# Moving one-hot comparisons and a rotation to GpSimd, taking softmax denominators from a ones column, and loading the output weights at a later point

## What is computed

```python
x = x + quantised_matmul(layernorm(x), ctx_4096)                 # L0 xattn
x = x + attention(layernorm(x), wq, bq, wk, bk, wv, bv)          # L0 attn: rotation of q and k, softmax(qk)v, 32 heads of 32
x = x + lora_ffn(layernorm(x), A, B, Wr)                         # L0 ffn: 64 experts, top 16, rank 16
x = x + knn_gather(ctx_4096[:, :2], layernorm(x), w, b)          # L1 xattn: 16 nearest of 1024 points, affine mix
x = x + causal_attention(layernorm(x), Wq, Wk, Wv) @ Wo          # L1 attn
x = x + lora_ffn1(layernorm(x), route_w, A, Bw)                  # L1 ffn: 8 experts, top 1
```

## Time and profile before

| | |
|---|---|
| median of 3 runs | 310.29 us (309.75 to 310.63) |
| profiled execution: device time | 308.52 us |
| profiled execution: span from first to last instruction | 306.7 us |
| PE busy | 221.6 us, 72% (1909 matmuls) |
| PEld busy | 135.4 us, 44% |
| DVE busy | 215.5 us, 70% (394 instructions) |
| ACT busy | 73.7 us, 24% |
| POOL busy | 26.4 us, 9% (29 instructions) |
| chain that ended last, by engine | PE 47%, DVE 34%, ACT 6%, issue 5%, DMA 4%, POOL 2% |
| mean granted TensorE clock | 0.80 of full speed |

### The profile page before, as it was taken

How to read it: one execution, slowest core, us unless ns; L and a number is a source line. 1 busy time by engine, 2 the same in 40 slices (tenths; PEclk the granted TensorE clock), 3 DMA queues, 4 the chain that set the end, 5 groups by cost and what they waited for, 6 DMA issues and landing times.

```text
span 306.7 us, 4506 instructions
## 1 busy us (share of the span) xinstructions
PE 221.6 (72%) x1909; PEld 135.4 (44%) x1909; DVE 215.5 (70%) x394; ACT 73.7 (24%) x112; POOL 26.4 (9%) x29
## 2 busy tenths in 40 slices
PE   0037443699997849669997993667729998989664
PEld 0021110333475727456444453667724476854251
DVE  0767997897998699989997978469860244911223
ACT  0439621100008235843217021000001013510010
POOL 7143470100000000010000001000010000000000
PEclk9999557559999756976999997775955999559976
DMA  4698999930004416606719674991000000000001
GB/s 135 183 332 300 370 416 343 388 151 0 2 0 139 138 51 191 178 0 235 316 40 409 248 266 156 362 410 39 6 0 0 0 0 2 2 2 0 0 0 68
DMA packets 18941, 45.09 MB, mean 147 GB/s; under 512 B 3829, under 2 KB 9079, under 8 KB 17898
## 3 DMA queue, kind: packets, MB, share of 16 engines
q1 hardware_dynamic: 17764, 44.12, 40.1%
q10 hardware_dynamic: 1158, 0.69, 0.8%
HBM read 44.16 MB, written 0.64 MB: 146 GB/s over the span
## 4 chain that ended last, share of the span: by engine, by line
PE 47%; DVE 34%; ACT 6%; issue 5%; DMA 4%; POOL 2%; SPq 1%; POOLq 0%; DVEq 0%
PE pair L352 16%; PE pair L547 5%; PE pair L491 5%; PE pair L527 4%; DVE knn_d L768 3%; DVE idx L763 3%; DVE idx L776 3%; DVE v L772 3%; DVE v L759 3%; PE pair L292 2%; DMA bufX<-in_ctx 2%; PE dist_ps L284 2%; DVE ring L809 2%; DVE bufY L847 2%; PE dist_ps L527 2%
## 5 line engine op out<-in xcount | busy, mean ns | idle before, releaser
L352 PE MATMUL pair<-are,xnT 128*128 128x256 f32 (+1 forms) x96 | 34.0, 502 | 0.0
L284 PE MATMUL dist_ps<-knn_rows 24*128 24x512 bf16 x32 | 11.6, 447 | 24.5 <-DMA knn_rows<-sq_scratch 20.1
L352 PEld LDWEIGHTS pair<-are,xnT 128*128 128x128 f32 x96 | 18.7, 204 | 13.9 <-issue 12.5
L1095 POOL TENSOR_SCALAR veps<-mv 128x1 f32<-128x1 f32 x6 | 1.4, 226 | 246.5 <-DVE mv L744 246.5
L759 DVE MAX8 v<-dist_ps 128x8 f32<-128x1024 f32 x16 | 19.5, 1221 | 3.7 <-PE dist_ps L284 3.6
L444 PE MATMUL pair<-arc,xnT 128*128 128x512 bf16 x32 | 14.0, 597 | 10.3 <-POOL arc L1103 9.6
L677 ACT COPY xnT<-pair 128x512 f32<-128x512 f32 x8 | 4.6, 586 | 69.5 <-PE pair L292 69.4
L292 PE MATMUL pair<-cst,xn 128*128 128x128 f32 x40 | 8.3, 376 | 16.5 <-DVE xn L750 16.5
L772 DVE MAX8 v<-knn_d 128x8 f32<-128x1024 f32 x16 | 19.5, 1221 | 0.2
L763 DVE FIND_INDEX8 idx<-v,dist_ps 128x8 uint32<-128x1024 f32 x16 | 19.6, 1223 | 0.0
L776 DVE FIND_INDEX8 idx<-v,knn_d 128x8 uint32<-128x1024 f32 x16 | 19.5, 1218 | 0.0
(11 more groups left out here) (171 smaller groups left out, 373.5 us busy)
## 6 DMA issues: line engine op xcount, KB each, us to landing
ring<-in_ctx SPq DMA_DIRECT2D x8, 1024.0 KB, 6.4
are<-in_L_attn_wq SPq DMA_DIRECT2D x1, 4096.0 KB, 14.9
ring<-in_L_ffn_A SPq DMA_DIRECT2D x4, 1024.0 KB, 13.4
are<-lo_scratch SPq DMA_DIRECT2D x4, 1024.0 KB, 7.7
ard<-in_L_attn_Wq SPq DMA_DIRECT2D x1, 4096.0 KB, 14.1
ring<-lo_scratch SPq DMA_DIRECT2D x4, 1024.0 KB, 4.7
arc<-in_L_attn_Wo SPq DMA_DIRECT2D x1, 4096.0 KB, 18.6
are<-in_L_attn_wk SPq DMA_DIRECT2D x1, 1024.0 KB, 17.4
```

Source lines behind the costliest of these rows:

```text
L284: m = mm(bank[h][:, :], q, knn_R[:, b, h * HALF:(h + 1) * HALF], start=True, stop=True)
L352: m = mm(o, xnTk[:, k, :], w(k), start=(l == 1 and k == 0), stop=(k == KT - 1))
```

## The change

- GpSimd now runs all eight `onehot` calls (same operation, same operands): 0 to 5 behind `power(2)`, then `power(3)`, then 6 and 7, then `power(4)` and `power(5)`.
- The rotation of L0 is on GpSimd, four `tensor_tensor` for each of three calls. ScalarE first copies q and k from PSUM into `xn`, the third copy behind the first rotation, whose input it overwrites. TensorE waits for the first of these copies before it reuses bank 4. L1 keeps its rotation on VectorE.
- V gets a 33rd column of ones in each of its 8 groups, so the product with the probabilities also gives their sum, in both layers. The reductions L864 and the reciprocal L867 go. Instead VectorE takes two reciprocals of 8 values from PSUM for each half of the heads, and the scaling is two `tensor_tensor` of 256 values where it was four of 128.
- SP waits for the sixth pick before it loads `Wo`.

```diff
             sp.wait_ge(sem("ffn0_filled"), 2)
+            sp.wait_ge(sem("picked"), PAIRS - 2)
             load(Wo, A["L1_attn_Wo"].rearrange("(k p) n -> p k n", p=P), "ld_wo")
...
                 if prep_a:
                     pe.wait_ge(sem("ld_wr"), 16)
+                    pe.wait_ge(sem("qk_copied"), 1)
...
                         g = 4 * (c // 2) + r
-                        o = (2 * g + c % 2) * DH
+                        o = (4 * (c // 2) + 2 * (r % 2) + c % 2) * OW
...
-                                       vsb[S * dup:S * dup + S, b, g * DH:(g + 1) * DH], start=True, stop=True)
+                                       vsb[S * dup:S * dup + S, b, g, :], start=True, stop=True)
...
+            for i, (o, n) in enumerate(((0, HALF), (HALF, HALF), (0, DKV))):
+                act.wait_ge(sem("k_filled") if i == 2 else sem("q_filled"), 1 if i == 2 else i + 1)
+                if i == 2:
+                    act.wait_ge(sem("rope_done"), 1)
+                cp(xn[:, o:o + n], bank[4 + i][:, 0:n]).then_inc(sem("qk_copied"), 1)
             attention(0, (0, 8, (2, 3)), (8, 8, (6, 7)))
...
                 for h in range(2):
-                    dve.wait_ge(sem("q_filled"), 2 * l + h + 1)
-                    rope(bank[4 + h], h * HALF, 4)
+                    if l:
+                        dve.wait_ge(sem("q_filled"), 2 * l + h + 1)
+                        rope(bank[4 + h], h * HALF, 4)
                     for t in mid[h]:
                         advance(t)
...
-                for r in range(4):
-                    dve.wait_ge(sem("probs_ready"), 4 * l + r + 1)
-                    ins = v.tensor_reduce(sdv[:, r], bufY[:, r * HALF:(r + 1) * HALF].rearrange("p (a j m) -> p a j m", a=2, j=4),
-                                          AX.X, ALU.add)
-                link(ins)
-                link(v.reciprocal(smx[:, :], sden[:, :]))
                 for t in late[1:]:
                     advance(t)
 
                 for n in range(2):
                     dve.wait_ge(sem("attn_filled"), 2 * l + n + 1)
...
                     for u in range(2):
-                        b = bank[(2 if n else 6) + u].rearrange("p (a n g d) -> p n a g d", a=2, n=2, g=4)[:, n]
-                        for a in range(2):
-                            ins = v.tensor_tensor(ov[:, a, :, u, :], b[:, a], rd[:, a, :, u].unsqueeze(2).to_broadcast([P, 4, DH]),
-                                                  ALU.mult)
+                        ins = v.reciprocal(rden[:, 2 * n + u, :], got[u][:, :, DH])
+                    link(ins)
+                    for u in range(2):
+                        ins = v.tensor_tensor(ov[:, u], got[u][:, :, 0:DH].rearrange("p (a g) d -> p a g d", a=2),
+                                              rden[:, 2 * n + u, :].rearrange("p (a g) -> p a g", a=2).unsqueeze(3)
+                                              .to_broadcast([P, 2, 4, DH]), ALU.mult)
...
             index_parts(3)
-            onehot(0)
...
             normalise(3)
-            onehot(1)
-            onehot(2)
-            onehot(3)
...
                 pick(p)
-                if p < 4:
-                    onehot(4 + p)
...
             g.memset(knn_R[:, :, :], 1.0).then_inc(sem("knn_rows_set"), 1)
+            g.memset(vsb[:, :, :, :].rearrange("p b g d -> p (b g d)"), 1.0).then_inc(sem("v_ones"), 1)
...
+            def onehot(q):
+
+                b, c = q // 4, q % 4
+                pool.wait_ge(sem(f"row_done{q}"), 16)
+                a = LOb[b][:, 4096 * c:4096 * c + 4096]
+                g.tensor_scalar(a, a, pcol, None, ALU.is_equal).then_inc(sem("onehot_ready"), 1)
...
-            for n in range(1, 6):
-                power(n)
+            power(1)
...
+                nc.gpsimd.tensor_tensor(a, ps, table(cosb, DH), ALU.mult).then_inc(sem("rope_part"), 1)
+                nc.gpsimd.tensor_tensor(dst[:, :, :, 0:hd], ps[:, :, :, hd:DH], table(sinb[:, 0:hd], hd), ALU.mult).then_inc(sem("rope_part"), 1)
+                nc.gpsimd.tensor_tensor(dst[:, :, :, hd:DH], ps[:, :, :, 0:hd], table(sinb[:, hd:DH], hd), ALU.mult).then_inc(sem("rope_part"), 1)
+                parts[0] += 3
+                pool.wait_ge(sem("rope_part"), parts[0])
+                nc.gpsimd.tensor_tensor(flat, flat, prod, ALU.add).then_inc(sem("rope_done"), 1)
+
+            for i, (o, n, j) in enumerate(((0, HALF, 4), (HALF, HALF, 4), (0, DKV, 1))):
+                pool.wait_ge(sem("qk_copied"), i + 1)
+                rope(xn[:, o:o + n], i * HALF, j)
+            power(2)
+            for q in range(6):
+                onehot(q)
+            power(3)
+            onehot(6)
+            onehot(7)
+            power(4)
+            power(5)
```

More of the change, by code:

```diff
@@ L28 @@
 DKV = KV * DH
+VW = DH + 1
+OW = DH + 2
 NPTS = 1024
@@ L111, in build @@
         rstd = sb("rstd", [P, 3])
-        smx = sb("smx", [P, H])
-        sden = sb("sden", [P, H])
+        rden = sb("rden", [P, 4, 8])
         v8 = sb("v8", [P, 4, 8])
@@ L872, in attention @@
                     dve.wait_ge(sem("attn_filled"), 2 * l + n + 1)
[L873 to L874 removed]
+                    ov = xn[:, :].rearrange("p (a n g u d) -> p n u a g d", a=2, n=2, g=4, u=2)[:, n]
+                    got = [bank[(2 if n else 6) + u][:, 0:8 * OW].rearrange("p (s d) -> p s d", d=OW) for u in range(2)]
                     for u in range(2):
[L876 to L879 removed]
+                        ins = v.reciprocal(rden[:, 2 * n + u, :], got[u][:, :, DH])
[4 more added lines that the diff above has]
+                                              .to_broadcast([P, 2, 4, DH]), ALU.mult)
                     if l:
```

30 lines of the change are left out of this document (17 added, 13 removed).

## The result

The changed kernel takes 352.47 us (median of 4 runs, 351.81 to 353.93) against 310.02 for the kernel before on the same chip: a ratio of 1.139, interval 1.132 to 1.145. It is 42 us slower; the forecast was 4.3 us slower, with a range that ended at 320. The profiled execution took 353.93 us, 45.4 more than the profiled execution of before.

A forecast was written before the change was run, and what follows sets the result against it. Bound by a chain: VectorE to 158.7 us, TensorE and ScalarE to 182, VectorE's norm and table, then TensorE's gather. Terms -1.95, +7.2, -1.4, +4.4, -4.2, +0.2 sum to +4.3 on 310.29: 314.6 us, range 303 to 320.

The forecast's parts named there:

- the length of a one-hot on GpSimd: GpSimd's 4096-value comparison, scaled from a 2048-value tensor_scalar of 1.90 us: 3.6 us, bounds 1.8 and 7.
- The third rival: Comparison on GpSimd slower: at 5 us each 323 us, at about 7 us each 335 us; chance 0.12.
- Rotation, 0: L0 rotation moved to GpSimd: ends by 91 us, ahead of `dist(7)`, so no gain or loss.
- Denominators in L0, -1.95: L0 attention: reductions and old reciprocal leave VectorE's chain, `xn` comes earlier; 1.95 us gained.
- One-hots 0 to 3, +7.2: GpSimd one-hots hold VectorE at L986 and the index split: +7.2 us, net +5.3 at `dist(14)`.
- One-hots 4 and 5, nothing: One-hots of pairs 4 and 5 on GpSimd end by 182, before `power(3)` at 190: no cost.
- Table, -1.4: Before the gather: one-hots 1 to 3 no longer stand between `xn` and the table copy; 1.4 us gained.
- One-hots 6 and 7, +4.4: On GpSimd after `power(3)`, they hold VectorE's norm and table, so the gather starts later: +4.4 us.
- Gather, -4.2: TensorE's gather stalls, read as instruction fetch beside loads, shrink from 7.6 to 3.4 us with `Wo` later; bounds 0 and 7.
- Denominators in L1, +0.2: L1 attention: TensorE can't use the earlier first half; new reciprocals follow the last product: +0.2 us.
- Blocking in one place only: Rival 2: VectorE blocked in one of two places, most likely at one-hots 0 to 3: 310.2 us; chance 0.12.
- hardly at all: Rival 1: blocking small, one-hots of 1.8 us or small instructions that pass: 303.0 us; chance 0.16.

The follow-up runs named there:

- the last two kernels: One-hots on VectorE where it waits, 0 to 4 ahead of the picks, three weight loads later: 300.21 us; the same with L0 rotation on VectorE, no ScalarE copies: 302.07 us.
- the first probe: Kernel before plus nine tensor_scalar forms on GpSimd at its end, on dead buffers; only lengths read: comparison 10.6 us, multiply and add 3.60 us.

## Why the prediction was wrong: one length, and one place without a term

**The step that failed** is the length of a one-hot on GpSimd: 3.6 us, with bounds of 1.8 and 7. It measured 10.6. The 3.6 was worked out from the 1.90 us of the earlier trace rows as if the tensor_scalar had one price whatever it computes. The arithmetic was exact: multiply and add over 4096 values does take 3.60 us. But a single comparison is another case, and even the upper bound, "twice the time of a multiply and add", had no row under it: no row of before shows a single-operation tensor_scalar of any size on GpSimd above 128x1. The Trainium skill, "GPSIMD Engine Reference", section "Performance pitfalls for Q7 kernels", was cited with 2.03 cycles a value, by estimate 7 us; that pointed the right way, and the measurement is half as much again.

**The rest of that sum at its own length, and at 10.6 us.** With one-hots of 3.7 us the changed kernel took 316.81 us, against 314.6. So near its own length the sum holds, and the mis-sized term is the length. The third rival priced longer one-hots: each microsecond above 3.6 counts six times. At 10.6 that is 6 x 7.0 = 42 us on 314.6, so 356.6 us, against 352.47 measured. That agreement is in good part luck. By this rule `dist(14)` would come 5.3 + 4 x 7.0 = 33.3 late, and it came 10.1 late, since VectorE waited there for the ends of two one-hots and not of four. One-hots 4 and 5, which the sum put at nothing, brought 18.4 instead. The norm was to bring 4.4 + 2 x 7.0 = 18.4 and brought 20.6. The mechanism, VectorE standing behind GpSimd's one-hots, is right; which of them count is right for short ones only.

Point by point:

- *Rotation, 0.* Right: with it and without it the last two kernels can't be told apart. On GpSimd the timeline has

```profile
71.59 1.26 POOL L1121 TENSOR_TENSOR bufZ<-xn,cst 128x512 f32<-128x512 f32 x1 [17.81 <-ACT xn L689]
...
87.00 0.73 POOL L1126 TENSOR_TENSOR bufX<-bufX,bufZ 128x256 f32<-128x256 f32 x1
```

So it ends at 87.7, ahead of `dist(7)`, as forecast. Its 1.26 us for 512 values are 2.0 ns a value behind the fixed 0.22, nearer to the upper of the two paces considered.
- *Denominators in L0, -1.95.* Right on its own (1.9, with L1 in it). In the changed kernel next to nothing of it arrived: the maximum that waits for `dist(13)` came at 144.45 instead of 145.5, and this execution was already 1.1 us ahead at a distance product that comes before the rotation (47.12 against 48.20). In the windows of 4 us from 128 to 144 the granted clock was 0.50 throughout, its lower level (1.2 GHz), where the kernel before had 0.80, 0.78, 0.65 and 0.50. The kernel with the denominators alone had 0.72, 0.85, 1.00 and 1.00 there. An earlier `xn` doesn't help where the products behind it take longer.
- *One-hots 0 to 3, +7.2, so +5.3 at `dist(14)`.* Blocking where it was said, at L986 and the index parts. `dist(14)` came 10.1 late. The index parts needed two ends of one-hots and not three: L986 was let go 1.8 us before the first end (last section), so the split met that same end, and the cast stood to the second.
- *One-hots 4 and 5, nothing.* Wrong, by the same length: "end by 182" became 206.4, and the index parts of groups 2 and 3 stood beside them (10.07, 10.53 and 3.51 us above). TensorE's transposes of `lof` wait for these and stand ahead of the ffn's products in its queue. This is the second loss of 18.4 us, in a place for which the prediction had no term. With one-hots of 3.7 us, numbers 4 and 5 ended at 185.1, the last split stood for 2.05 us, and neither transpose made TensorE wait, so "nothing" was right for the length that was assumed.
- *Table, -1.4.* There, but covered: from the table product to the gather 5.15 us instead of 4.97, with the product itself 1.56 longer at the lower clock.
- *One-hots 6 and 7, +4.4.* Mechanism right, and here both stood in the path whole: 20.6 us at `xn`. Putting them behind the table gave 20 back.
- *Gather, -4.2.* 26.5 us instead of 32.0, so -5.5; the stalls kept are 2.59 and 0.19, where 2.6 and twice 0.2 were forecast. By these terms 7.6 becomes 3.0 and not 3.4, so the term should have been -4.6; a fourth stall of 0.50 (at 217.59) went as well. That `Wo` is the cause is shown by the run in which only `Wo` moved. That the stalls are a fetch of instructions was not shown: it rests on their distance of 256 instructions and on their going when the DMAs go.
- *Denominators in L1, +0.2.* The output product behind the attention started 43.9 late (317.00 against 273.08), with 43.8 ahead of the stage: 0.1. The last 1.3 us of the span's 45.2 come behind it.

**The rivals.** Blocking in one place only or hardly at all is refuted by the `xn` row and the casts. The third, a slower comparison, is what happened, at a chance of 0.12 and with a price that still fell short. The range left most of it out, since its upper end was set by the 2.5 us of the norm and the gather's gain, and the one unknown that six instructions multiplied got a chance instead of width.

## What to carry to other kernels

A price holds for the operation and the form in which it was measured; where the trace has only a multiply and add, a lone comparison on GpSimd is unknown, and its error is to be multiplied by the number of such instructions on the path before the range is drawn. Count moved work against what stands beside it: GpSimd's idle time is free beside VectorE instructions that read PSUM or search for maxima, and dear beside casts, integer splits and norms, however small they are. And look for idle stretches on the engine that already does the work well: four of the eight one-hots of 1.28 us, put where VectorE waited, were worth 1.3% together with two later loads, where moving all eight off cost 16% against the same kernel with them on VectorE.

## What the runs showed of the hardware

- GpSimd's tensor_scalar over 128x4096 values has three prices: 3.6 us (multiply and add, multiply twice, minimum and maximum), 10.5 to 10.7 (any single operation that was tried: comparison, multiply, add), 14.0 to 14.4 (comparison, add or subtract first in a pair). bf16 or f32, in place or not, constant or per-partition operand change it by 0.1 us, or 0.4 in the pair with a comparison. VectorE's comparison takes 1.28 us.
- A VectorE instruction that meets a GpSimd instruction of 5 to 10 us stands inside its own busy time: a cast, integer tensor_scalar or `xn` to GpSimd's very end; a tensor_tensor on two SBUF operands until 1.8 to 1.9 us before that end (L986: free at 151.60, the one-hot until 153.5; L806: free at 154.57, GpSimd until 156.43). This early release was seen beside comparisons only: beside the multiply and add of the earlier trace rows, L948 stood until 44.49, and GpSimd's instruction ended at 44.47. Maxima, index searches, and picks from PSUM aren't held. Nor are instructions on one value for each partition (L989 in a one-hot, 0.16 us; a cast in the first probe, 0.15). The Trainium skill, "SBUF — State Buffer", section "Who interferes with whom", names the same two classes; the early release and the small ones that pass are from these rows only.
- Beside GpSimd comparisons of 2.84 us VectorE lost almost nothing: a tensor_tensor was held for the first 1.0 us, and casts, splits and even a one-hot of 1.28 us that came between 1.0 and 1.7 us into one passed. Splits that came 1.9 us or more into one stood to its end. The dummy beside such a one-hot took 3.5 to 3.9 us itself. What happens inside GpSimd's instruction to open this gap was not tried.
- TensorE can stand still with nothing to wait for while bulk loads run: 7.6 us in a gather of 32 beside 381 GB/s, 1.92 with the last load moved, none in the first 288 of the products into the pairs with all three moved.
